# One wait of GpSimd for four places of the gather ring, in both gather layers and both attentions of a graph network

## What is computed

```python
# layer 0: dot-product attention along the edges, 8 heads of 32
q, k, v = h @ Wq + bq, h @ Wk + bk, h @ Wv + bv
p = segment_softmax(sum_d(q[src] * k[dst]) / sqrt(32), dst)
out0 = segment_sum(v[src] * p, dst)
# layer 1: mean of the neighbours, by dst and by src, into a GRU cell
agg_in  = segment_mean((h @ W_in.T + b_in)[src], dst)
agg_out = segment_mean((h @ W_out.T + b_out)[dst], src)
out1 = gru(concat(agg_in, agg_out), h)
# layer 2: relational mean, 8 edge types
hW = einsum('nd,rde->rne', h, weight)
out2 = h @ sl_w.T + sl_b + segment_sum(hW[edge_type, src], dst) / deg
# layer 3: additive attention (GAT), 8 heads, then a batch norm
e = leaky_relu(a_src[src] + a_dst[dst])
out3 = batchnorm(segment_sum(xh[src] * segment_softmax(e, dst), dst) + bias)
```

## Time and profile before

| | us |
|---|---|
| median of 3 runs | 8363.24 |
| runs | 8353.29 to 8367.53 |
| the profiled execution | 8371.75 |
| span of the profiled execution | 8370.0 |
| PE, DVE, POOL, ACT busy in the span | 6094.9, 5551.2, 4456.5, 1651.8 |

### The profile page before, as it was taken

How to read it: one execution, slowest core, us unless ns; L and a number is a source line. 1 busy time by engine, 2 the same in 40 slices (tenths; PEclk the granted TensorE clock), 3 DMA queues, 4 the chain that set the end, 5 groups by cost and what they waited for, 6 DMA issues and landing times. The chain is left out here.

```text
span 8370.0 us, 94632 instructions
## 1 busy us (share of the span) xinstructions
PE 6094.9 (73%) x24717; PEld 3487.7 (42%) x24717; DVE 5551.2 (66%) x13040; ACT 1651.8 (20%) x5142; POOL 4456.5 (53%) x4606
## 2 busy tenths in 40 slices
PE   1497777777737667778888799967777667777774
PEld 1245555555524333334444444433333344444442
DVE  8678888888886776444444444444444677777777
ACT  0122222222220000000000045500000244444441
POOL 1004444444437777777777711177777255555550
PEclk9998888888869999999999999999999977777776
DMA  0255555555553333354444544433333533333343
GB/s 7 70 193 152 150 153 152 153 151 149 152 153 100 94 96 100 104 114 130 134 129 134 132 146 167 156 110 104 104 104 105 137 101 99 102 100 101 102 99 98
DMA packets 446242, 1012.45 MB, mean 121 GB/s; under 512 B 98363, under 2 KB 213607, under 8 KB 439072
## 3 DMA queue, kind: packets, MB, share of 16 engines
q0 software_dynamic: 240960, 702.53, 31.7%
q1 hardware_dynamic: 204768, 303.99, 11.0%
HBM read 845.66 MB, written 160.28 MB: 120 GB/s over the span
## 5 line engine op out<-in xcount | busy, mean ns | idle before, releaser
L691 PE MATMUL psum<-rows,oh 128*128 128x257 f32 (+2 forms) x8800 | 3091.5, 453 | 1273.4 <-issue 407.1
L691 PEld LDWEIGHTS psum<-rows,oh 128*128 128x128 f32 x8800 | 1620.7, 212 | 2651.4 <-issue 894.4
L698 DVE TENSOR_TENSOR acc<-acc,psum 128x264 f32 (+2 forms) x3520 | 1490.9, 424 | 1298.8 <-PE psum L691 1167.7
L670 POOL DMA_INDIRECT rows<-qv_tab,src_i x880 | 845.8, 961 | 1470.0 <-PE psum L691 699.2
L670 POOL DMA_INDIRECT rows<-xh_tab,src_i x880 | 833.6, 947 | 775.6 <-PE psum L691 455.9
L787 PE MATMUL psum<-ident,ones 128*128 128x512 bf16 x3069 | 1176.8, 414 | 0.0
L670 POOL DMA_INDIRECT rows<-h_tab,src_i x880 | 904.9, 1028 | 291.0 <-PE psum L691 143.8
L670 POOL DMA_INDIRECT rows<-h_tab,wts x880 | 872.6, 992 | 268.1 <-PE psum L691 142.3
L670 POOL DMA_INDIRECT rows<-hw_tab,rel_i x880 | 848.7, 964 | 283.7 <-PE psum L691 210.2
L698 DVE TENSOR_TENSOR kh<-kh,psum 128x257 f32 x880 | 371.7, 422 | 632.0 <-PE psum L691 620.2
L847 PE MATMUL psum<-kh,oht 128*128 x1760 | 632.8, 495 | 1.3 <-ACT oht L959 1.3
(11 more groups left out here) (331 smaller groups left out, 7315.8 us busy)
## 6 DMA issues: line engine op xcount, KB each, us to landing
wts<-hots SPq DMA_DIRECT2D x220, 256.0 KB, 3.6
hw_tab<-acc SPq DMA_DIRECT2D x50, 1024.0 KB, 4.1
part_tab<-rows SPq DMA_DIRECT2D x50, 512.0 KB, 3.6
rows<-part_tab SPq DMA_DIRECT2D x50, 512.0 KB, 5.5
hots<-oh SPq DMA_DIRECT2D x74, 256.0 KB, 2.8
rows<-qv_tab,src_i POOLq DMA_INDIRECT x880, 3.7
rows<-h_tab,src_i POOLq DMA_INDIRECT x880, 2.8
rows<-h_tab,wts POOLq DMA_INDIRECT x880, 2.8
```

What stands on the lines that cost most here:

```text
L670: nc.gpsimd.indirect_dma_start(rows[:, b, 0:width], None, table, bass.IndirectOffsetOnAxis(index, 0)).then_inc(ring[b], 16)
L691: nc.tensor.matmul(psum[:, banks[b % len(banks)], 0:width], oh[:, b // GROUP, b % GROUP], rows[:, b, at:at + width], start=True, stop=True ...
L698: nc.vector.tensor_tensor(to, to, psum[:, banks[b % len(banks)], 0:width], ALU.add).then_inc(acc_done, 1)
```

## The change

`gather` gets a parameter `together`. With 4, only the gathers into places 0, 4, 8 and 12 wait, and they wait until the last of the four places that follow is free. The other three of four wait for nothing. All five stages use 4.

```diff
-    def gather(pool, j, b, table, width, index):
-        pool.wait_ge(agg_done, prev(j, b, RING))
+    def gather(pool, j, b, table, width, index, together=1):
+
+        if b % together == 0:
+            pool.wait_ge(agg_done, prev(j, b + together - 1, RING))
         nc.gpsimd.indirect_dma_start(rows[:, b, 0:width], None, table,
                                      bass.IndirectOffsetOnAxis(index, 0)).then_inc(ring[b], 16)
...
-                    gather(pool, j, b, table, width, src_i[:, s:s + 1])
+                    gather(pool, j, b, table, width, src_i[:, s:s + 1], together=4)
...
-            gather(pool, K1 + n // RING, n % RING, h1_tab, D, index[:, s:s + 1])
+            gather(pool, K1 + n // RING, n % RING, h1_tab, D, index[:, s:s + 1], together=4)
...
-            gather(pool, K2 + n // RING, n % RING, hw_tab, D, rel_i[:, n:n + 1])
+            gather(pool, K2 + n // RING, n % RING, hw_tab, D, rel_i[:, n:n + 1], together=4)
```

## The result

The changed kernel takes 8494.23 us (median of four runs, 8485.81 to 8501.33) against 8358.76 us before (8353.29 to 8367.53): a ratio of 1.0157, 95% interval 1.0145 to 1.0169. It is 135 us slower. The prediction said 7790 us, and the range up to 8450 did not hold the result.

What follows compares the result with a forecast made beforehand. GpSimd was taken to bound the gather layers, with removable 0.305 us gaps. 8371.75 - 576 (gaps) + 2 (attention 2) = 7798, less 8.5 from profiled execution to median: 7790 us, range 7720 to 8450.

Steps and rivals of the forecast that it cites:

- GpSimd bounds the gather layers: Both layer 1 passes and layer 2: GpSimd never really stops; 880 slots of 1.269 us make layer 2's 1116 us.
- the one long wait a group: Attentions: half or more of GpSimd's idle 1470.0 and 775.6 us is one wait a group, 3.88 and 5.97 us.
- The gap belongs to the wait: Gather layers: the 0.305 us between gathers comes from a DMA having a wait, and goes with the wait; chance 0.60.
- the 576 us that the sum took off: Both gather layers: gains of 593 us together, less 12 us for slowed gathers and 5 us for the sort stretch.
- the addition with two satisfied waits: GpSimd's L1845 started with no gap; the prediction read a wait as such as free, but not a DMA with one.
- Gains of 201, 191 and 201 us in the passes: Layer 1's first and second pass and layer 2: 660 removed waits each at 0.305 us, the second pass stopped by PE.
- The later start in the layers and in attention 1 costs nothing: Layers: some ten ring slots to spare; attention 1: start under 3 us later, 6.6 us free; cost nothing.
- Attention 2: Later start mostly hidden, as 1.49 us are free before the scan; 2 us allowed in all if the gap goes.
- rival 1: The gap stays, layers gain nothing, attention 2's gathers come late: 81 us slower, 8444 us; chance 0.30.
- The late start was put at 2.97 us: Attention 2: first gather waits for slot 3's addition at 7180.34 in place of slot 0's at 7177.37.
- half the excess: Attention 2, rival 1: 1.48 us reach the scan, the period grows by 0.74 us, times 110 groups 81 us.
- The range: Whole kernel: 7720 to 8450 us, covering both signs; the main case's own range was 7720 to 7880.

Runs made afterwards that it cites:

- the fillers: Four more filler matmuls a group in attention 2, between maxima and sums on TensorE: ratio 0.9997 in the kernel before, 1.0160 in the changed kernel, second chip.
- slot 2: Kernel before, but each group's first gather in attention 2 waits for slot 2's release: ratio 1.0213 on the third chip, 1.0045 on the fourth.
- slot 4: Kernel before, but each group's first gather in attention 2 waits for slot 4's release: ratio 1.0138 on the third chip, 1.0444 on the fourth.

## Why the prediction was wrong

**GpSimd bounds the gather layers:** right. Each pass is 880 times 1.27 to 1.33 us with no gap over 0.31 us in layer 2, and with direct DMAs layer 2 fell from 1256 to 739 us on the second chip. (That the one long wait a group is half of GpSimd's idle time holds for attention 2; in attention 1 it is 5.97 x 110 = 657 of 1470 us.)

**The gap belongs to the wait:** the step that failed, and with it the 576 us that the sum took off. It was read from L1411, a direct DMA with a wait and 0.29 us of idle time before it. But that DMA had waited for an instruction which ended just then; 0.29 us is what passes from a release to a start. It says nothing on a wait that was long over. The row that spoke to the point was the addition with two satisfied waits and no gap, which the prediction saw and set aside. "Nothing else sets gathers and direct DMAs apart in that" was the weak sentence: they are different instructions, and 0.305 us is the gather's own, with or without a wait.

**Gains of 201, 191 and 201 us in the passes:** measured 5, 0 and -3 us by the windows; all but attention 2 together, -5 us with an interval that reaches +1.

**The later start in the layers and in attention 1 costs nothing:** right. The windows keep 1732, 1140 and some 1119 us, and the change without attention 2 is at 0.9993. That is the first chip; on the second attention 1 was shorter with the change and the fillers.

**Attention 2:** rival 1 named the mechanism and the place, and the sign was its. Its size, 81 us for 135, came from two terms. The late start was put at 2.97 us, since slot 3's addition was taken to stay where the earlier trace rows had it; measured were 3.96 us in place of 0.26 after slot 0, 3.70 later, since the release itself moved. And the period was let grow by half the excess, as if one full period lay between a late start and the next; measured, it grew by 1.20 us in place of 0.74. On TensorE the turn of the scores stands ahead of the sums of slots 2 and 3. Once it waits for the landing, it holds back the very release for which the next gathers wait. The earlier trace rows already had the way home: from L969 at 7175.66 to slot 3's addition at 7180.34, with L853 at 7178.01: 2.33 us lie between L853 and the addition, and the 2.35 us ahead of L853 are TensorE's other work, which a late landing would wait out. The rows of after give what was missing: L855 0.36 us behind L971 (7513.99 to 7514.35), the gather 0.13 us behind the addition, and 2.98 us from the last gather's start to L971 (7511.01 to 7513.99). The way home is 0.36 + 2.33 + 0.13 = 2.82 us, and with seven starts of 1.25 us the ring is 8.75 + 2.98 + 2.82 = 14.55 us, 1.10 over the period of 13.45, or 121 us.

**The range** ended at 8450 because rival 1's price stood in it as one number, with no upper bound of its own.

## What to carry to other kernels

A small gap ahead of an instruction tells what a wait costs only if that wait was already over; look for one that was. When waits are bundled and the start moves to a later release, follow that release back: if it hangs on something that needs the transfer being started, there is a ring, and its whole length is the new period, not the old period plus the delay. A release can be taken off such a ring by moving what stands ahead of it on its engine: here that took the price of the late start from 135 to 5 us and cost 28 us itself. And a ratio that comes out as expected on another chip proves nothing until its stages do too.

## What the runs showed of the hardware

- Two gathers of 128 rows start at least 1.24 us apart on GpSimd, 1.25 in the median (0.946 busy, 0.305 idle), with or without a wait between; 64 rows 1.20 us. Direct DMAs of 128 rows start 0.54 us apart.
- A write of 0.12 us between two gathers costs nothing: it lies in the 0.305 us.
- A satisfied wait ahead of a DMA on GpSimd costs nothing that the trace can show (18 direct DMAs with one each in 9.68 us).
- On two of four chips TensorE's results reached VectorE 1.5 to 1.7 us (medians) after the last matmul's start in place of 0.30, and 4.6 and 4.8 us with other timing around it, at a granted clock of 0.82 to 0.84 over the run in place of 0.87 to 0.89. What holds them is open; in the kernel before the fillers did not change it (1.7 us with and without). A dose measured there (slot 2 worse than slot 4) turned round on another chip.
